# Banded attention on one core: output products and values moved behind the next group's projections

## What is computed

```python
q = rope(x @ wq.T)   # 16 heads of 128
k = rope(x @ wk.T)   # 4 key/value heads of 128
v = x @ wv.T
scores = qg . k * scale                       # qg: 4 query heads to each key/value head
allowed = (s <= t) & (t - s <= 128)
probs = softmax(where(allowed, scores, min))
x = x + (probs . v) @ wo.T
```

## Time and profile before

| | |
|---|---|
| median of 3 runs | 2412.54 us (2406.25 to 2413.64) |
| the profiled execution, own time | 2406.55 us |
| its span in the profile | 2404.8 us |
| the stage of the change in it | PE works on it from 14.9 to 926.7 us |
| busy in the span | PE 89%, DVE 71%, ACT 39%, POOL 44% |

### The profile page before, as it was taken

One profiled execution on the slowest core, in us unless ns is written; L12 is line 12 of the kernel. 1 busy time (PEld: TensorE's weight loads), 2 busy tenths in 40 slices (PEclk: granted clock), 3 DMA queues, 4 the chain that ended last, 5 costly groups with the idle time before them and its releaser, 6 DMA issues. The chain is left out here.

```text
span 2404.8 us, 24923 instructions
## 1 busy us (share of the span) xinstructions
PE 2151.0 (89%) x7344; PEld 1108.7 (46%) x7344; DVE 1712.6 (71%) x2983; ACT 944.7 (39%) x1808; POOL 1048.7 (44%) x798
## 2 busy tenths in 40 slices
PE   6998999899999977997889898999789999999858
PEld 2554445454455543443555555465333433334234
DVE  1787788768876885786889889889546364654554
ACT  1443344333333433764655646465123232332311
POOL 2343354333333440322899998999511011010142
PEclk9999999999999998998999999999889999999979
DMA  7000000000000002455644526353332122221121
GB/s 263 19 19 18 19 20 20 18 18 22 22 18 19 23 23 90 159 186 214 266 162 166 197 105 210 127 203 108 107 80 78 41 77 57 70 70 46 52 109 53
DMA packets 95563, 214.87 MB, mean 89 GB/s; under 512 B 15832, under 2 KB 33112, under 8 KB 93032
## 3 DMA queue, kind: packets, MB, share of 16 engines
q1 hardware_dynamic: 77192, 156.18, 19.8%
q10 hardware_dynamic: 17760, 57.42, 6.7%
q0 software_dynamic: 512, 0.13, 0.0%
HBM read 146.30 MB, written 42.07 MB: 78 GB/s over the span
## 5 line engine op out<-in xcount | busy, mean ns | idle before, releaser
L759 POOL TENSOR_SCALAR a_prob<-a_prob,a_rsum 128x256 f32<-128x256 f32 x256 | 146.6, 590 | 467.3 <-DVE a_rsum L687 467.1
L1455 POOL TENSOR_TENSOR s_state<-s_b_rows,s_delta_u 128x1024 f32<-128x1024 f32 x128 | 303.5, 2384 | 36.9 <-DMA s_b_rows<-scan_bc 34.4
L1499 DVE TENSOR_TENSOR_SCAN s_state<-s_decay,s_state 128x512 f32<-128x512 f32 x256 | 304.9, 1211 | 15.5 <-ACT s_decay L1441 13.2
L1614 PE MATMUL c_bank<-c_xn_parts,c_w_parts 128*128 128x512 f32 (+1 forms) x1056 | 269.5, 405 | 6.2 <-DMA c_w_parts<-ffn_weights_lo 6.2
L1441 ACT ACTIVATE s_decay<-s_delta,s_a 128x512 f32<-128x512 f32 x256 | 173.5, 689 | 226.1 <-DVE s_state L1499 220.6
L491 PE MATMUL a_bank<-a_xn_t,a_wq 128*128 128x512 f32 x512 | 227.3, 592 | 0.0
L602 ACT ACTIVATE a_prob<-a_score,a_neg_m 128x256 f32<-128x256 f32 x256 | 117.6, 475 | 279.0 <-DVE a_neg_m L682 278.8
L1614 PEld LDWEIGHTS c_bank<-c_xn_parts,c_w_parts 128*128 128x128 f32 (+1 forms) x1056 | 196.3, 187 | 65.8 <-issue 20.3
L574 PE MATMUL a_bank<-a_wo,a_out_t 128*128 128x512 f32 x512 | 222.3, 593 | 0.0
L2049 ACT ACTIVATE d_prob_t<-d_score 128x512 f32<-128x512 f32 x256 | 138.9, 595 | 192.2 <-PE d_score L1931 191.1
L373 DVE TENSOR_SCALAR f_picks<-f_mask,f_lut_xor,f_lut 128x260 int32<-128x260 int32 x512 | 202.3, 468 | 9.6 <-DVE f_mask L367 0.5
(11 more groups left out here) (210 smaller groups left out, 3646.2 us busy)
## 6 DMA issues: line engine op xcount, KB each, us to landing
s_b_rows<-scan_bc SPq DMA_DIRECT2D x64, 512.0 KB, 3.7
c_w_parts<-ffn_weights_hi ACTq DMA_DIRECT2D x39, 512.0 KB, 3.6
c_w_parts<-ffn_weights_lo ACTq DMA_DIRECT2D x39, 512.0 KB, 4.5
f_idx<-in_idx SPq DMA_DIRECT2D x64, 130.0 KB, 2.1
ffn_weights<-f_picks SPq DMA_DIRECT2D x64, 130.0 KB, 1.8
d_qs<-d_hi SPq DMA_DIRECT2D x128, 64.0 KB, 2.0
d_ks<-d_hi SPq DMA_DIRECT2D x128, 64.0 KB, 2.0
d_factor<-in_factors SPq DMA_DIRECT2D x16, 512.0 KB, 3.6
```

The source lines that it names most:

```text
L1455: pool.tensor_tensor(self.state[:, s], row.broadcast_to([P, 2, T]), self.delta_u[:, h % 2], ALU.mult) \
L1499: dve.tensor_tensor_scan(self.state[:, s, e, :], self.decay[u % 2][:], self.state[:, s, e, :], 0.0, ALU.mult, ALU.add).then_inc(self.scann ...
L1614: mm = nc.tensor.matmul(banks[b][0:width[o], :], w_parts[:, n % SLOTS, w, at:at + width[o]], xn_parts[:, x_, k, :], start=((k, w, x_) == t ...
```

## The change

PE's order in a group becomes: two heads' scores, `k` and `q0`, the other two heads' scores, `q1` to `q3`, then the output products of the group before, then transposes and `weigh`. The first group has the values in the place of output products. The last group has its own output products behind that. In its first part stand, when another pass follows, the features and the third group's output products. The values leave the first ring. DVE's adds for a group therefore stand in the next group's row of work, between the lookups, and the lookups are dealt out as 4, 4, 3, 5 to the four groups. The norm's last part (`norm_apply`) stands behind the adds. The diff, cut (ACT's and POOL's orders follow PE's in the same way):

```diff
+    GROUPS = (0, 4, 8, 11, PER_PASS)
...
             def one_pass(i, more):
-                for g in range(KV):
...
+                for g in range(LAST):
                     scores(i, g, (0, 1))
-                    if ng == 0 and more:
-                        ring.wait_free(pe, i, consumed=xn_steps)
-                    project(ring, i, ng, nxt[0:2])
-                    scores(i, g, (2,))
-                    project(ring, i, ng, nxt[2:3])
-                    scores(i, g, (3,))
-                    project(ring, i, ng, nxt[3:])
...
+                    project(ring, i, g + 1, proj(g + 1)[0:2])
+                    scores(i, g, (2, 3))
+                    project(ring, i, g + 1, proj(g + 1)[2:])
+                    if g:
+                        outputs(i, g - 1)
+                    else:
+                        values(i)
+                    weighted(i, g)
+                scores(i, LAST, (0, 1))
                 if more:
-                    values(ring, i)
+                    norm_tensor(nc, pe, norm, consts.ident, ring, banks, i + 1, in_pass=i)
+                    outputs(i, LAST - 1)
+                    scores(i, LAST, (2, 3))
+                    ring.wait_free(pe, i, consumed=xn_steps)
+                    project(ring, i, 0, proj(0))
+                else:
+                    scores(i, LAST, (2, 3))
+                    outputs(i, LAST - 1)
+                weighted(i, LAST)
+                outputs(i, LAST)
...
-            values(first, 0)
-            first.wait_free(pe, 0, consumed=proj(0) + v_steps)
+            first.wait_free(pe, 0, consumed=proj(0))
...
+            def take_output(i, g, tt):
+
+                if g:
+                    add(i, g - 1, tt)
+                elif tt % 2 == 0:
+                    take(("v", tt), i, v[:, tt, :])
...
+                    if g == LAST - 1 and more:
                         wait_apart(dve, x_in, 16 * (B - 1), waited)
-                        norm_vector(nc, dve, norm, x, i + 1)
...
+                        norm_stats(nc, dve, norm, x, i + 1)
+                    lookup.pick(i, chunks[1])
+                    take_output(i, g, 0)
+                    lookup.choose(i, chunks[1])
+                    take_output(i, g, 1)
+                    lookup.pick(i, chunks[2])
+                    take_output(i, g, 2)
+                    take_output(i, g, 3)
+                    if g == LAST - 1 and more:
+                        norm_apply(nc, dve, norm, x, i + 1)
+                    lookup.choose(i, chunks[2])
+                    for n in chunks[3:]:
+                        lookup.pick(i, n)
+                        lookup.choose(i, n)
```

More of the change, by code:

```diff
@@ new lines, in outputs @@
+            def outputs(i, g):
+                pe.wait_ge(w_in["wo"], 16)
+                for tt in range(TT):
+                    ring.wait_free(pe, i, ("wo", g, tt), consumed=[("pv", g, tt)])
+                    b, _ = ring.at(("wo", g, tt), i)
+                    for r in range(REPS):
+                        mm = nc.tensor.matmul(banks[b][:], out_t[:, tt, r * P:(r + 1) * P],
+                                              wo[:, g * REPS + r, :],
+                                              start=(r == 0), stop=(r == REPS - 1))
+                    mm.then_inc(ring.full[b], 1)
@@ new lines, in one_pass @@
+            def one_pass(i, more):
+                for g in range(LAST):
+                    at = (ring, i, i, g + 1)
+                    exponentials(i, g, (0, 1))
+                    swap(*at, proj(g + 1)[0:2])
+                    exponentials(i, g, (2, 3))
+                    swap(*at, proj(g + 1)[2:])
+                    if g == 0:
+                        values(i)
+                    weighted(i, g)
+                exponentials(i, LAST, (0,))
+                if more:
+                    features(ring, i)
+                exponentials(i, LAST, (1, 2, 3))
+                if more:
+                    swap(ring, i, i + 1, 0, proj(0))
+                weighted(i, LAST)
@@ new lines, in one_pass @@
+                lookup.pick(i, chunks[0])
+                add(i, LAST - 1, 0)
+                lookup.choose(i, chunks[0])
+                add(i, LAST - 1, 1)
+                lookup.pick(i, chunks[1])
+                add(i, LAST - 1, 2)
+                add(i, LAST - 1, 3)
+                if more:
+                    maxima(i, h + 2)
+                    maxima(i, h + 3)
+                inverse(i, h + 2)
+                lookup.choose(i, chunks[1])
+                inverse(i, h + 3)
+                at = (ring, i, i + 1, 0)
@@ new lines, in one_pass @@
+                if more:
+                    rope(*at, proj(0)[0:2])
+                lookup.pick(i, chunks[2])
+                if more:
+                    rope(*at, proj(0)[2:3])
+                lookup.choose(i, chunks[2])
+                if more:
+                    rope(*at, proj(0)[3:])
+                lookup.pick(i, chunks[3])
+                lookup.choose(i, chunks[3])
+                lookup.pick(i, chunks[4])
+                add(i, LAST, 0)
+                lookup.choose(i, chunks[4])
@@ L734, in _ @@
+                for tt in range(1, TT):
+                    add(i, LAST, tt)
             norm_vector(nc, dve, norm, x, 0)
```

153 lines of the change are left out of this document (65 added, 88 removed).

## The result

| | before | change |
|---|---|---|
| median | 2410.86 us (7 runs, 2406.25 to 2415.50) | 2423.35 us (7 runs, lowest 2418.93) |
| ratio | | 1.0048, interval 1.0031 to 1.0065 |
| the profiled execution, own time / span | 2406.55 / 2404.8 us | 2423.73 / 2422.0 us |
| PE works in the stage to | 926.7 us | 938.65 us |

The forecast was 2401 and 62% for faster; the change costs 12.5 us by the medians. The stage itself is 11.9 us longer. (Behind it the changed profile is 5.2 us longer too, in code that the change does not touch; the medians, which differ by the stage's 12 alone, do not bear that out. One execution of the change was disturbed, 2606 us, and is left out of the ratio.)

A forecast was written before the change was run, and what follows sets the result against it. PE, issuing nearly back to back, was taken as the bound. Three passes -11.5, last pass -5 and first ring +5.2 summed to -11.3 us: 2401 on the median 2412.54, range 2387 to 2414, chance of faster 0.62.

The forecast's parts named there:

- The bound and the chain: PE bounds the stage; its waits for probabilities go, and transposed banks reusing output banks wait for DVE's late adds.
- the last stop: Last pass's last group: PE waits 6.6 us for the last probability, after DVE's two picks and two chooses.
- clock loss: Behind PE's stops: 0.8 us each for waits of 3.2 and 3.3, half of a full loss of 1.3 to 2.
- At waits near 2.8 the trace shows full rate: PE's transposes behind a wait of 2.80 us: no clock loss, while a wait of 6.48 shows half rate.
- clock at every stop: Rival: each of 15 bank stops costs 1.5 us of clock, 22 in all, giving 2417 us; chance 0.24.
- The first group's 1.1: PE's wait at the third transposed bank in a pass's first group, where the values stand: 1.1 us.
- A small lateness is taken up by DVE's own waits for ACT: DVE reaches the next maxima on time by 0.2 us; waits such as 2.26 before the last rope product absorb lateness.
- The fourth group's 2.6 + 0.7: Fourth group, another pass following: waits of 2.4 and 0.2 us at transposed banks, 0.7 for `choose` beside POOL (bound 0 to 2).
- The third group's 3.2: PE's wait at the third transposed bank in the third group, statistics ahead of the first `pick`: 3.2 us.
- The first ring: Program's start: without the values the gap before the first scores is bare, first pass starts at 50.4; cost +5.2 us.
- DVE did not become the bound: Rival: second `pick` slowed, wait grows 3.3 us in groups one to three, DVE late to maxima; 2437 us, chance 0.11.
- the adds come in time: Rival: first `pick` does not suffer, only third and fourth groups' waits are left; -26 us, time 2387, chance 0.14.

The follow-up runs named there:

- adds_first: The change with the third and fourth add of the first three groups ahead of the second `pick`: 2395.69 us, 0.9951 of before.
- the fillers: The change with two or three unused products per group ahead of the third transposed bank: 2414.22 and 2418.78 us, 1.0021 and 1.0041 of before.
- unrolled: The change with the four passes written out instead of a loop of three and a last one: 2416.28 us, 1.0038 of before.
- outputs_only: The change without its move of the values, which stay at a pass's end and in the first ring: 2457.89 us, 1.0201 of before.

## Why the prediction was wrong

**The bound and the chain were right.** The 15 waits for probabilities and the features' wait went, DVE's adds became the releaser at the third transposed bank, and the last stop was 6.55 for a forecast of 6.6. adds_first shows the cause by taking it away in the first two groups.

**The step that failed first: clock loss.** "For waits of 3.2 and 3.3 I take a loss of 0.8 each", and nothing at 2.8 or less. Measured behind stops were 3.6, 4.9 and 5.0 in the three passes instead of 1.6 each, and 5.7 in the last pass instead of 2.2. Two things were wrong in it. "At waits near 2.8 the trace shows full rate" rested on one row, and the same stop in the two passes beside it had a stretch at half rate behind it. And half of what a full loss cost was too little: behind the stops of 4.17 it was 2.3 (10.60 instead of 8.25 in the same work), and even stops of 2.08 in the last pass lost 1.9. The rival "clock at every stop" priced the loss behind stops at 22 us; 19.2 were measured. That this is so near is partly luck. Its rule isn't right as it stood, since none of the stops under 1.9 us cost clock and those near 2.1 went either way, but the stops of 4.17 cost more than its 1.5 and made up for them. I had given it 24%, and nearly all of that to a loss of half as much, without a row for the half. The Trainium skill (TensorE: Matmul & The Clock Gate, "A second HAM failure mode: psum-queue depth-cycling") says that short idle times made by going round PSUM banks make the clock swing. The trace agrees for the longer stops of this case, and the fillers show it; the 46 stops under 1.9 us did not do it.

**The second: stops, 2.2 us a pass.** The first group's 1.1 was 2.8 in passes two and three. "A small lateness is taken up by DVE's own waits for ACT" failed: the loop's jump made DVE 1.1 late, and the wait for ACT grew with it, from 2.26 to 3.73, since ACT's swap itself waited for POOL, and POOL for DVE. A wait for an engine that is in turn waiting for oneself has no slack in it. The fourth group's 2.6 + 0.7 was 4.17: the mechanism, `choose` beside POOL, was named, and its size set near the wrong end of 0 to 2. The third group's 3.2 was 3.3 in the first pass and 2.7 in the others.

**The first ring: right in its mechanism, 3.2 short in size.** It was +8.4 for +5.2. The half rate behind the idle 14 us was 2.4 for a forecast of 2. The first scores started at 53.22 and not at 50.4, and 2.1 of this is the `k` projection, which took 5.81 us instead of 3.67; in adds_first and unrolled, where it took 3.67, they started at 50.9 and 50.7. As the same code takes either time, these 2.1 us are the luck of the profiled execution and not the change's.

**The other rivals.** DVE did not become the bound; nothing of the 3.3 us a group was seen. But outputs_only shows how near that was: without the values in the first group DVE is late to the next maxima, with stops of 8 us. That the adds come in time was not so.

## What to carry to other kernels

When work of PE is moved so that probabilities are no longer late, write down for every PSUM bank behind it who empties it and what stands ahead of that instruction on its engine; the new stop is there. Price a stop of PE with the clock that it may take as well as its length, and treat a length seen once at full rate as open: in this stage the clock behind stops cost 19.2 us in the change and some 14 before, where the stops were fewer and longer. Where a stop can't be removed, moving work that is needed anyway into it (the next scores) pays twice.

## What the runs showed of the hardware

- Half rate followed none of 46 stops of 0.3 to 1.9 us, 21 of 29 from 2.3 to 2.9, and all 22 over 3.7. Between 1.9 and 2.3 it followed 9 of 26 in nine kernels and 7 of 8 in three others, and in one kernel it followed one pass's stop and not the next pass's of the same length. Filling the stops with 27 us of unused products made the kernel 7 to 9 us faster.
- At a loop's jump back 2.40 us lay between DVE's last add and its next maxima, with no wait in the trace. With the passes written out 1.27 us lie between them, a wait for PE's scores, so that the jump made the maxima some 1.1 us late.
- Seven `COPY_PREDICATED` of 128x260 took 4.87 us beside POOL's two-input work and 3.0 alone; POOL's sum took 2.33 instead of 1.3.
- Loads issued by ACT held back its own work: issued by SP, the first scores came 13.4 us earlier (2.1 of it from a faster `k` projection), and a load needed early that then stood behind them made DVE wait 6.4 us.
- The `k` projection at the program's start took 3.67 us in six of the fourteen profiled executions and 5.4 to 6.1 in eight, whatever the edit. In before and in the change the granted clock reads 1.00 over it, so no row here says why.
